# A ViT block on one NeuronCore: mask and row maximum in one VectorE instruction per head, in a reordered pipeline

## The chip, the cores and the metric

One NeuronCore of a Trainium2 chip runs the whole program; the other cores are idle. The metric is the device time of one execution in microseconds (us). Below, PE is TensorE, DVE is VectorE, ACT is ScalarE, POOL is GpSimd and SP is the engine that issues all DMAs. Each engine works through its own queue in order; semaphores tie the queues together.

## The reference: what is computed

Sixteen images of 256 by 256 pixels go through one block. The input is (16, 3, 256, 256) in fp32.

```python
gray  = einsum('bchw,c->bhw', x, (0.2989, 0.587, 0.114))
edges = conv 3x3 of gray with 2 Scharr filters, 'SAME'
h = abs(edges).sum(axis=1) / 2                       # (16, 256, 256)
xn = layernorm(h)                                    # no weights, eps 1e-5
Q = (xn @ W_dq @ W_uq) ; K = (xn @ W_dkv @ W_uk) ; V = (xn @ W_dkv @ W_uv)   # 16 heads of 16
scores = Q K^T / 4, causal, softmax over keys        # 256 x 256 per head
h = h + (softmax(scores) @ V) @ W_o
h = h + layernorm(h) @ sign(W_ffn).T
```

## The kernel before, in words

The unit of work is one image: 256 rows, as T = 2 tiles of 128 partitions. The 16 heads go in NG = 4 groups of G = 4. Queries and keys are cut into three bf16 parts each and stored so that six part products lie along the contraction (96 rows, KQ); three further rows (up to KM = 99) carry the row maximum, also in three parts, so that it is subtracted inside the product.

For each group the kernel does two things.

- **Query-major**, to find the maximum of each row: `hi_scores` (L836) gives queries 128 to 255 against all 256 keys, 4 heads, 1024 columns in two PSUM banks; `lo_scores` (L851) gives queries 0 to 127 against keys 0 to 127, 512 columns. A further product of a bf16 identity with a mask tile (`mask_qk`, L838 and L853) adds -3e38 above the diagonal. DVE then takes one `tensor_reduce` over 4 heads: `max_hi` (L668) and `max_lo` (L674). POOL cuts the maxima of 8 heads into parts (`cut_max`), PE transposes them (`turn_max`), ACT copies them and SP writes them into the operand (`load_max_rows`).
- **Key-major**, one image later: `key_scores_first` (L867, mask L869) and `key_scores_second` (L886), for keys 0 to 127 and 128 to 255. The second block has no mask product; DVE applies it with a minimum against a tile, in place in PSUM (`cap`, L679). ACT takes the exponential (`exp_first` L529, `exp_second` L534). `values` (L897, L900) multiplies with V, which carries a column of ones, so that the sum comes out too. ACT copies the result (L540), PE transposes it (`turn_output`, L926), DVE inverts the sums and multiplies (`normalize`, L686 and L689), PE transposes again (`turn_attn`), ACT copies (L545).

Around it stand, per image: gray (ACT L484, DVE L637 and L640), a store and a shifted reload through HBM, the filters (`filters`, L784), `both_edges` (ACT L490), the sum and statistics (DVE `sum_edges`, L646 to L654), the first normalization (POOL, L432 to L442), its transpose (`turn_x`), `compress` (L798), `expand_qk` (L807), `expand_v` (L817), the cut into parts (ACT L506 and L510, DVE L660, POOL `third_part` L462), a store and six reloads per half (`store_parts`, `load_operands`), and at the end `project` (L771), `add_y` (DVE L696 to L704), the second normalization (POOL, L447 to L457), `turn_y`, `feed_forward` (L771) and `add_z` (L709).

The order is written out by hand: a software pipeline over a step `i`, in which each engine works on several images at once. In step i, PE does scores of image i, key-major scores and values of i-1, the end of attention for i-2, projection for i-3, feed-forward for i-4, and the preparation of i+2 and i+3. Each step has four phases, one per head group.

## Time and profile before

| what | value |
|---|---|
| time, median of 3 runs | 512.27 us (504.1 to 512.48) |
| time of the profiled execution | 510.29 us |
| its span, first to last instruction | 508.4 us |
| mean granted TensorE clock | 0.946 of full speed |
| PE busy | 395.0 us (78%) |
| DVE busy | 289.1 us (57%) |
| ACT busy | 230.7 us (45%) |
| POOL busy | 163.7 us (32%) |
| DMA | 74.06 MB, mean 146 GB/s |

The profiled execution is 2.0 us under the median, and 1.9 us of it lie outside the span. Busy PE time is that of pipelined matmuls whose ends are modelled, so it overstates how full PE is.

### The profile page before, as it was taken

The numbers are of one execution on the slowest core, as the hardware profiler recorded it, in microseconds if no ns is written. First come the engines' busy times: TensorE is split into PE (matmuls) and PEld (weight loads), VectorE is DVE, ScalarE is ACT, GpSimd is POOL, SyncE is SP. The second block draws the span as 40 slices with busy tenths as digits, with TensorE's granted clock in tenths as the row PEclk, the third lists the DMA queues.
The fourth block names the chain that finished last, engine by engine and source line by source line (L and its number), as shares of the span: only waits on it lengthen the run. The fifth ranks groups of instructions, "written<-read, shape, count | busy, mean of one in ns | idle before, by whom it ended". The sixth has DMA issues, their size and how long they took to land.

```text
span 508.4 us, 10109 instructions
## 1 busy us (share of the span) xinstructions
PE 395.0 (78%) x3736; PEld 284.2 (56%) x3780; DVE 289.1 (57%) x508; ACT 230.7 (45%) x385; POOL 163.7 (32%) x363
## 2 busy tenths in 40 slices
PE   0047448586979898989898989898989899889863
PEld 0023335455656666666666666666666667666542
DVE  1422255574736667676666767676757576664321
ACT  2013123363635555555555555555555554446400
POOL 8220331413122424242424242424242422220111
PEclk9999569797979999999999999999999999999977
DMA  5954797675655666666767676737372425200000
GB/s 157 259 130 93 220 255 168 177 181 180 165 158 134 180 176 169 179 169 186 171 177 181 177 174 178 194 95 194 100 189 68 147 68 185 85 24 24 21 22 21
DMA packets 72186, 74.06 MB, mean 146 GB/s; under 512 B 6379, under 2 KB 65995, under 8 KB 72139
## 3 DMA queue, kind: packets, MB, share of 16 engines
q1 hardware_dynamic: 72138, 73.42, 53.6%
q8 instruction: 31, 0.51, 0.4%
q14 instruction: 17, 0.13, 0.1%
HBM read 51.97 MB, written 21.04 MB: 144 GB/s over the span
## 4 chain that ended last, share of the span: by engine, by line
PE 24%; POOL 23%; issue 22%; DVE 6%; ACT 1%; POOLq 0%
PE bank L771 9%; POOL parts L462 5%; POOL xn L442 4%; PE bank L764 3%; POOL yn L457 3%; PE bank L867 2%; POOL rstd L449 2%; DVE y L696 2%; PE bank L798 2%; PE bank L836 2%; POOL rstd L434 2%; DVE stats L700 1%; POOL max_rest L422 1%; POOL max_parts L427 1%; POOL max_parts L425 1%
## 5 line engine op out<-in xcount | busy, mean ns | idle before, releaser
L668 DVE TENSOR_REDUCE neg_max<-bank 128x4 f32<-128x1024 f32 x64 | 78.1, 1220 | 47.6 <-PE bank L838 46.6
L529 ACT ACTIVATE probs<-bank 128x1024 f32<-128x1024 f32 x64 | 65.6, 1025 | 63.3 <-PE bank L869 63.1
L462 POOL TENSOR_TENSOR parts<-rest,parts 128x1024 bf16<-128x1024 f32 x16 | 34.0, 2125 | 144.3 <-ACT parts L510 144.3
L784 PE MATMUL bank<-rows,band 102*32 102x256 f32 x512 | 34.3, 413 | 26.6 <-DMA rows<-gray_padded 25.7
L679 DVE TENSOR_TENSOR bank<-bank,cap_kq 128x512 f32<-128x512 f32 x64 | 44.4, 694 | 15.5 <-PE bank L886 15.5
L534 ACT ACTIVATE probs<-bank 128x512 f32<-128x512 f32 x64 | 38.2, 597 | 32.7 <-DVE bank L679 32.4
L836 PE MATMUL bank<-k_st,q_st 96*128 96x256 bf16 x256 | 48.6, 284 | 4.2 <-ACT edge L490 1.8
L867 PE MATMUL bank<-q_st,k_st 99*128 99x256 bf16 x256 | 47.5, 279 | 1.8 <-issue 0.2
L447 POOL TENSOR_SCALAR var<-mv 128x2 f32<-128x2 f32 x16 | 3.5, 219 | 133.3 <-DVE mv L704 133.3
L771 PE MATMUL bank<-w_sign,yn_t 128*128 128x256 f32 x128 | 35.1, 422 | 12.1 <-issue 9.9
L674 DVE TENSOR_REDUCE neg_max<-bank 128x4 f32<-128x512 f32 x64 | 43.6, 681 | 0.0
L764 PE MATMUL bank<-ident,xn 128*128 128x128 f32 x64 | 13.2, 341 | 37.5 <-POOL xn L442 37.5
L660 DVE TENSOR_TENSOR rest<-bank,parts 128x512 f32<-128x512 f32 x32 | 20.6, 686 | 35.8 <-ACT parts L506 35.8
L897 PE MATMUL bank<-probs,v_ring 128*32 128x256 f32 x512 | 40.6, 389 | 0.0
L540 ACT COPY o_un<-bank 128x256 f32<-128x256 f32 x64 | 23.6, 369 | 33.4 <-PE bank L900 33.4
L784 PEld LDWEIGHTS bank<-rows,band 102*32 102x32 f32 x512 | 16.3, 117 | 38.8 <-issue 30.5
L838 PE MATMUL bank<-mask_qk,ident_bf 128*128 128x256 bf16 x128 | 36.4, 285 | 0.0
L869 PE MATMUL bank<-mask_kq,ident_bf 128*128 128x256 bf16 x128 | 35.8, 280 | 0.0
L771 PEld LDWEIGHTS bank<-w_sign,yn_t 128*128 128x128 f32 x128 | 25.1, 207 | 18.2 <-issue 11.8
L771 PE MATMUL bank<-w_out,a_t 128*128 128x256 f32 x128 | 31.3, 387 | 1.4 <-ACT a_t L545 1.3
L867 PEld LDWEIGHTS bank<-q_st,k_st 99*128 99x128 bf16 x256 | 24.4, 100 | 13.0 <-issue 5.5
L490 ACT ACTIVATE edge<-bank 128x1024 f32<-128x1024 f32 x16 | 16.4, 1025 | 33.5 <-PE bank L784 33.5
(95 smaller groups left out, 768.8 us busy)
## 6 DMA issues: line engine op xcount, KB each, us to landing
x_sb<-in_x SPq DMA_DIRECT2D x16, 768.0 KB, 6.0
rows<-gray_padded SPq DMA_DIRECT2D x48, 256.0 KB
qk_parts<-parts SPq DMA_DIRECT2D x16, 768.0 KB, 4.1
q_st<-qk_parts SPq DMA_DIRECT2D x96, 128.0 KB, 3.9
k_st<-qk_parts SPq DMA_DIRECT2D x96, 128.0 KB, 3.6
gray_padded<-gray SPq DMA_DIRECT2D x16, 258.0 KB, 3.4
out_dram<-z SPq DMA_DIRECT2D x16, 256.0 KB, 2.5
rows<-gray_padded SPq DMA_DIRECT2D x32, 24.0 KB
```

What stands on the lines that cost most here:

```text
L462: pool.tensor_tensor(parts[:, n % 2, SLOTS_OF_PART[2], :, :], rest[:, :, :, :], parts[:, n % 2, SLOTS_OF_PART[1], :, :], ALU.subtract).the ...
L529: nc.scalar.activation(probs[:, g, :, 0:S], ps_k0, ACT.Exp, scale=SCALE).then_inc(exp0_done, 1)
L534: nc.scalar.activation(probs[:, g, :, S:S + P], ps_k1, ACT.Exp, scale=SCALE).then_inc(exp1_done, 1)
L668: nc.vector.tensor_reduce(neg_max[:, 1, heads], ps_hi, AX.X, ALU.max, negate=True).then_inc(max_hi_done, 1)
L674: nc.vector.tensor_reduce(neg_max[:, 0, heads], ps_lo, AX.X, ALU.max, negate=True).then_inc(max_lo_done, 1)
L679: nc.vector.tensor_tensor(ps_k1, ps_k1, cap_kq[:, :].unsqueeze(1).to_broadcast([P, G, P]), ALU.min).then_inc(capped, 1)
L771: last = nc.tensor.matmul(dst[:, t, :], src_t[:, c, t * P:(t + 1) * P], w[:, c, :], start=(c == 0), stop=(c == T - 1))
L784: last = nc.tensor.matmul(ps_edge[b * RB:(b + 1) * RB, t, f, :], band[0:KC, f, :], rows[0:KC, n % 2, t * (P // RB) + b, :], start=True, st ...
L836: nc.tensor.matmul(ps_hi[:, b * two + i, :], q[:, hh, P:S], k[:, hh, :], start=(i == 0), stop=False, skip_group_check=True)
L838: last = nc.tensor.matmul(ps_hi[:, b * two:(b + 1) * two, P:S], ident_bf[:, :], mask_qk[:, 0:two, :], start=False, stop=True, skip_group_c ...
L867: nc.tensor.matmul(ps_k0[:, i, :], k[:, hh, 0:P], q[:, hh, :], start=(i == b * two), stop=False, skip_group_check=True)
L897: nc.tensor.matmul(ps_o[i * VW:(i + 1) * VW, :], v_ring[:, n % V_RING, 0, g * G + i, :], probs[:, g, i, 0:S], start=True, stop=False, skip ...
```

## The change

Six things change together.

1. The mask products of the query-major scores go. Instead DVE runs one `tensor_tensor_reduce` per head: it adds a fp32 tile `mask_low` to the scores in place and gives the maximum of each row. That is 4 instructions in `max_hi` (256 columns each) and 4 in `max_lo` (128 each).
2. The mask of the second key block becomes a product on PE with `mask_kq` (512 columns) and `cap` goes.
3. After `values`, DVE transposes in blocks of 32 by 32 straight from PSUM (`turn_values`), inverts the sums, POOL multiplies (`normalize`), and DVE transposes back (`turn_attn`) into the operand of `project`. Heads are numbered by `head_of` so that this fits. PE's `turn_output` and `turn_attn` and ACT's five copies go.
4. The sum of the two edges moves from DVE to POOL. Both applications of the normalization (`xn`, `yn`) move from POOL to ACT. `both_edges` becomes two instructions, of half size.
5. PSUM: the small products now lie in banks 6 and 7 and no longer share banks with the scores, except for the filters, which still lie in the two banks of `ps_hi`.
6. The order of every queue changes and the tail is shorter: the attention of an image ends one step earlier, its projection too, and its feed-forward.

The new orders in step i (numbers in brackets are the image; a bar parts the phases):

- PE: key scores 0 [i-1], hi 0, lo 0 [i], values 3 [i-2], expand_v [i+1], turn_max 1 [i-1], turn_y [i-3] | key scores 1, hi 1, lo 1, values 0 [i-1], feed_forward [i-3], turn_x [i+2] | key scores 2, hi 2, lo 2, values 1 [i-1], project [i-2], turn_max 0 [i], compress [i+2] | key scores 3, hi 3, lo 3, values 2 [i-1], filters [i+3], expand_qk [i+2].
- DVE: rest_of_parts [i+1], max_hi 0, turn_values 3 and invert 1 [i-2], max_lo 0, measure_h [i+2] | max_hi 1, turn_values 0 [i-1], max_lo 1, turn_attn 1 [i-2] | rest_of_gray [i+4], add_z [i-3], max_hi 2, turn_values 1 and invert 0 [i-1], max_lo 2 | add_y [i-2], max_hi 3, turn_values 2 and turn_attn 0 [i-1], max_lo 3.
- ACT: exponentials 0 [i-1], second_part and copy_v [i+1], max rows 1 [i-1], copy_yt [i-3], normalize_x [i+2] | exponentials 1, first_gray [i+4], copy_xt [i+2] | exponentials 2, max rows 0 [i], copy_c [i+2] | exponentials 3, both_edges [i+3], normalize_y [i-2], first_part [i+2].
- POOL: cut_max 1 [i-1], sum_edges and scale_x [i+2], normalize 1 [i-2], third_part [i+1], cut_max 0 [i], normalize 0 [i-1], scale_y [i-2].
- SP: load_rows [i+3], max rows 1 [i-1], store_parts and load_operands 0 [i+1], store_z [i-3], max rows 0 [i], store_gray [i+4], load_x [i+6], load_operands 1 [i+1]. The weights are loaded behind the first rows, no longer ahead of the first gray image.

In the diff the common indent is cut, and lines left out are marked.

```diff
--- before.py
+++ after.py
...
-FIRST = -6
-LAST = IMAGES + 4
+FIRST = -4
...
+def head_of(g, i):
+    return (g // 2) * HALF + g % 2 + 2 * i
...
+    def sum_edges(n):
+        pool.wait_ge(abs_done, T * (n + 1))
+        need(pool, y_done, upto(n - H_RING))
+        need(pool, xn_done, T * upto(n - H_RING))
+        pool.tensor_tensor(h_ring[:, n % H_RING, :, :], edge[:, :, 0, :], edge[:, :, 1, :],
+                           ALU.add).then_inc(h_done, 1)
...
+    def scale_x(n):
...
+        pool.tensor_scalar(less[:, :], mv[:, :, 0], -1.0, None, ALU.mult).then_inc(less_done, 1)
...
+        pool.wait_ge(less_done, n + 1)
+        pool.tensor_tensor(shift[:, :], less[:, :], rstd[:, :], ALU.mult).then_inc(shift_done, 1)
...
+    def normalize(n, c):
+        k = T * n + c + 1
+        pool.wait_ge(recip_done, k)
+        need(pool, at_done, k - T)
+        pool.tensor_tensor(attn[:, c, :, :, :].rearrange("p q x d -> p x q d"), u[:, c, :, :, 0:DK],
+                           recip[:, c, :, :].unsqueeze(3).to_broadcast([P, 2, NQ, DK]),
+                           ALU.mult).then_inc(attn_done, 1)
...
     def both_edges(n):
-        act.wait_ge(filters_done, T * (n + 1))
         need(act, h_done, n)
-        nc.scalar.activation(edge[:, :, :, :], ps_edge, ACT.Abs).then_inc(abs_done, 1)
+        for t in range(T):
+            act.wait_ge(filters_done, T * n + t + 1)
+            nc.scalar.activation(edge[:, t, :, :], ps_edge[:, t, :, :], ACT.Abs).then_inc(abs_done, 1)
+    def normalize_x(n):
+        act.wait_ge(shift_done, n + 1)
+        need(act, xt_done, n)
+        for t in range(T):
+            nc.scalar.activation(xn[:, t, :], h_ring[:, n % H_RING, t, :], ACT.Identity,
+                                 bias=shift[:, t:t + 1], scale=rstd[:, t:t + 1]).then_inc(xn_done, 1)
...
     def exp_second(n, g):
         at = NG * n + g
-        act.wait_ge(capped, at + 1)
+        act.wait_ge(k1_done, at + 1)
...
-    def copy_o(n, g):
-        act.wait_ge(o_done, NG * n + g + 1)
-        if g == 0:
-            need(act, ot_done, T * (n - 1))
-        nc.scalar.copy(o_un[:, n % 2, g, :], ps_o).then_inc(o_copied, 1)
-    def copy_at(n):
-        act.wait_ge(at_done, n + 1)
-        need(act, proj_done, n)
-        nc.scalar.copy(a_t[:, :, :], ps_at).then_inc(at_copied, 1)
...
     def max_hi(n, g):
-        heads = slice(g * G, (g + 1) * G)
         if g % 2 == 0:
             need(dve, cut[1], 2 * n - 1 + g // 2)
         dve.wait_ge(hi_done, NG * n + g + 1)
-        nc.vector.tensor_reduce(neg_max[:, 1, heads], ps_hi, AX.X, ALU.max,
-                                negate=True).then_inc(max_hi_done, 1)
+        for i in range(G):
+            last = nc.vector.tensor_tensor_reduce(ps_hi[:, i, :], ps_hi[:, i, :], mask_low[:, :], 1.0, MASK,
+                                                  ALU.add, ALU.max,
+                                                  top[:, 1, g // 2, i, g % 2].unsqueeze(1))
+        last.then_inc(max_hi_done, 1)
     def max_lo(n, g):
-        heads = slice(g * G, (g + 1) * G)
         dve.wait_ge(lo_done, NG * n + g + 1)
-        nc.vector.tensor_reduce(neg_max[:, 0, heads], ps_lo, AX.X, ALU.max,
-                                negate=True).then_inc(max_lo_done, 1)
-    def cap(n, g):
-        dve.wait_ge(k1_done, NG * n + g + 1)
-        nc.vector.tensor_tensor(ps_k1, ps_k1, cap_kq[:, :].unsqueeze(1).to_broadcast([P, G, P]),
-                                ALU.min).then_inc(capped, 1)
-    def normalize(n, t):
-        k = T * n + t + 1
-        o = ps_ot.rearrange("p (h d) -> p h d", d=VW)
-        dve.wait_ge(ot_done, k)
-        nc.vector.reciprocal(recip[:, t, :], o[:, :, DK]).then_inc(recip_done, 1)
-        dve.wait_ge(recip_done, k)
-        need(dve, at_done, n)
-        nc.vector.tensor_tensor(attn[:, t, :].rearrange("p (h d) -> p h d", d=DK), o[:, :, 0:DK],
-                                recip[:, t, :].unsqueeze(2).to_broadcast([P, H, DK]),
-                                ALU.mult).then_inc(attn_done, 1)
+        for i in range(G):
+            last = nc.vector.tensor_tensor_reduce(ps_lo[:, i, :], ps_lo[:, i, :], mask_low[:, P:S], 1.0, MASK,
+                                                  ALU.add, ALU.max,
+                                                  top[:, 0, g // 2, i, g % 2].unsqueeze(1))
+        last.then_inc(max_lo_done, 1)
+    def turn_values(n, g):
+        c, x = g // 2, g % 2
+        dve.wait_ge(o_done, NG * n + g + 1)
+        need(dve, attn_done, T * (n - 1) + c + 1)
+        nc.vector.transpose(u[:, c, x, :, :].rearrange("p q d -> p (q d)"), ps_o).then_inc(o_turned, 1)
+    def invert(n, c):
+        dve.wait_ge(o_turned, NG * n + 2 * c + 2)
+        nc.vector.reciprocal(recip[:, c, :, :], u[:, c, :, :, DK]).then_inc(recip_done, 1)
+    def turn_attn(n, c):
+        dve.wait_ge(attn_done, T * n + c + 1)
+        need(dve, proj_done, n - 1)
+        nc.vector.transpose(a_t[:, n % 2, c, :],
+                            attn[:, c, :, :, :].rearrange("p q x d -> p (q x d)")).then_inc(at_done, 1)
...
-        need(pe, y_done, upto(n - 6))
-        need(pe, z_done, upto(n - 7))
...
     def turn_x(n):
         pe.wait_ge(xn_done, T * (n + 1))
-        need(pe, attn_done, T * upto(n - 5))
-        need(pe, v_copied, n)
+        need(pe, o_turned, NG * upto(n - 4) + (1 if live(n - 3) else 0))
+        need(pe, rest_done, 2 * n)
         turn(ps_xt, xn, xt_done)
...
     def expand_qk(n):
         pe.wait_ge(c_copied, n + 1)
-        need(pe, exp0_done, NG * upto(n - 4) + (3 if live(n - 3) else 0))
-        need(pe, rest_done, 2 * n)
+        need(pe, o_turned, NG * upto(n - 4) + (3 if live(n - 3) else 0))
+        need(pe, v_copied, upto(n - 1))
+        need(pe, y_done, upto(n - 4))
...
     def expand_v(n):
         pe.wait_ge(c_copied, n + 1)
-        need(pe, attn_done, T * upto(n - 5) + (1 if live(n - 4) else 0))
...
         need(pe, max_hi_done, NG * n + g)
         if g == 0:
-            need(pe, abs_done, upto(n + 2))
-        if g == 1:
-            need(pe, z_done, upto(n - 4))
-        if g == 2:
-            need(pe, y_done, upto(n - 3))
-        for b in range(2):
-            for i in range(two):
-                hh = g * G + b * two + i
-                nc.tensor.matmul(ps_hi[:, b * two + i, :], q[:, hh, P:S], k[:, hh, :],
-                                 start=(i == 0), stop=False, skip_group_check=True)
-            last = nc.tensor.matmul(ps_hi[:, b * two:(b + 1) * two, P:S], ident_bf[:, :],
-                                    mask_qk[:, 0:two, :], start=False, stop=True,
-                                    skip_group_check=True)
+            need(pe, abs_done, T * upto(n + 2))
+        for i in range(G):
+            hh = head_of(g, i)
+            last = nc.tensor.matmul(ps_hi[:, i, :], q[:, hh, P:S], k[:, hh, :], start=True, stop=True)
         last.then_inc(hi_done, 1)
     def lo_scores(n, g):
         q = q_st[0:KQ, n % 2, :, :]
         k = k_st[0:KQ, n % 2, :, :]
         need(pe, max_lo_done, NG * n + g)
-        if g == 1:
-            need(pe, at_copied, upto(n - 3))
         for i in range(G):
-            hh = g * G + i
-            nc.tensor.matmul(ps_lo[:, i, :], q[:, hh, 0:P], k[:, hh, 0:P],
-                             start=(i == 0), stop=False, skip_group_check=True)
-        nc.tensor.matmul(ps_lo[:, :, :], ident_bf[:, :], mask_qk[:, :, :], start=False, stop=True,
-                         skip_group_check=True).then_inc(lo_done, 1)
+            hh = head_of(g, i)
+            last = nc.tensor.matmul(ps_lo[:, i, :], q[:, hh, 0:P], k[:, hh, 0:P], start=True, stop=True)
+        last.then_inc(lo_done, 1)
...
-        if g == 0:
-            need(pe, yt_copied, upto(n - 3))
         if g == 1:
             need(pe, mt_copied, 2 * (n + 1))
         if g == 3:
             need(pe, mt_copied, 2 * (n + 1) + (1 if live(n + 1) else 0))
         for i in range(G):
-            hh = g * G + i
-            last = nc.tensor.matmul(ps_k1[:, i, :], k[:, hh, P:S], q[:, hh, P:S],
-                                    start=True, stop=True)
-        last.then_inc(k1_done, 1)
+            hh = head_of(g, i)
+            nc.tensor.matmul(ps_k1[:, i, :], k[:, hh, P:S], q[:, hh, P:S],
+                             start=(i == 0), stop=False, skip_group_check=True)
+        nc.tensor.matmul(ps_k1[:, :, :], ident_bf[:, :], mask_kq[:, :, :], start=False, stop=True,
+                         skip_group_check=True).then_inc(k1_done, 1)
...
             pe.wait_ge(v_copied, n + 1)
         pe.wait_ge(exp1_done, at + 1)
-        need(pe, o_copied, at)
+        need(pe, o_turned, at)
+        if g == 0:
+            need(pe, yt_copied, upto(n - 2))
+        if g == 1:
+            need(pe, xt_copied, upto(n + 3))
+        if g == 2:
+            need(pe, c_copied, upto(n + 3))
+        if g == 3:
+            need(pe, rest_done, 2 * upto(n + 3))
         for i in range(G):
...
-    def turn_output(n, t):
-        if t == 0:
-            pe.wait_ge(o_copied, NG * (n + 1))
-            need(pe, c_copied, upto(n + 4))
...
-                                       o_un[:, n % 2, g, t * P:(t + 1) * P], ident[:, :])
-        last.then_inc(ot_done, 1)
-    def turn_attn(n):
-        pe.wait_ge(attn_done, T * (n + 1))
-        need(pe, max_lo_done, NG * upto(n + 2) + (1 if live(n + 3) else 0))
-        turn(ps_at, attn, at_done)
     def project(n):
-        pe.wait_ge(at_copied, n + 1)
-        need(pe, max_hi_done, NG * upto(n + 2) + (2 if live(n + 3) else 0))
+        pe.wait_ge(at_done, T * (n + 1))
         need(pe, z_done, upto(n - 1))
-        need(pe, abs_done, upto(n + 5))
-        product(ps_y, a_t, w_out, proj_done)
+        need(pe, v_copied, upto(n + 3))
+        product(ps_y, a_t[:, n % 2, :, :], w_out, proj_done)
...
     def turn_y(n):
         pe.wait_ge(yn_done, T * (n + 1))
-        need(pe, exp1_done, NG * upto(n + 2))
+        need(pe, o_turned, NG * upto(n + 1))
         turn(ps_yt, yn, yt_done)
```

## Rows read from the trace of the kernel before

**Rows 1.** Chain that ended last, in time order: start us, us, what; two steps.

```profile
243.37 2.12 POOL parts L462
...
253.90 1.80 PE bank L771 x8
...
269.17 2.12 POOL parts L462
```

**Rows 2.** Windows: us, busy (x instructions) of PE, PEld, DVE, ACT, POOL; clock, DMA, GB/s.

```profile
0.00:67.60 67.60, 23.82 (x150) 13.66 (x151) 19.65 (x39) 14.20 (x21) 23.46 (x41) 0.92 0.67 175
...
202.80:301.60 98.80, 87.66 (x902) 63.98 (x912) 68.51 (x122) 55.19 (x93) 37.76 (x84) 1.00 0.68 180
...
457.00:508.40 51.40, 36.47 (x270) 25.24 (x268) 16.19 (x36) 14.68 (x25) 8.20 (x22) 0.87 0.06 22
```

**Rows 3.** Groups by line, DVE: count, busy us, mean ns, idle before.

```profile
L668 DVE TENSOR_REDUCE neg_max<-bank 128x4 f32<-128x1024 f32 x64 | 78.1, 1220 | 47.6 <-PE bank L838 46.6
...
L679 DVE TENSOR_TENSOR bank<-bank,cap_kq 128x512 f32<-128x512 f32 x64 | 44.4, 694 | 15.5 <-PE bank L886 15.5
L674 DVE TENSOR_REDUCE neg_max<-bank 128x4 f32<-128x512 f32 x64 | 43.6, 681 | 0.0
...
L689 DVE TENSOR_TENSOR attn<-bank,recip 128x256 f32<-128x256 f32 x32 | 13.6, 424 | 1.2
...
L646 DVE TENSOR_TENSOR h_ring<-edge 128x512 f32<-128x512 f32 x16 | 11.1, 692 | 35.5 <-ACT edge L490 35.5
```

**Rows 4.** Timeline, DVE: start us, us, instructions, idle before. Pairs without a wait between.

```profile
256.44 0.75 DVE L700 BATCH_NORM_STATS2 stats<-y 128x6 f32<-128x256 f32 x2
257.12 0.30 DVE L704 BATCH_NORM_AGGREGATE mv<-stats 128x2 f32<-128x6 f32 x2
```

**Rows 5.** Groups by line: the small DVE operations that pair up in rows 4.

```profile
L700 DVE BATCH_NORM_STATS2 stats<-y 128x6 f32<-128x256 f32 x32 | 12.0, 418 | 0.5
...
L704 DVE BATCH_NORM_AGGREGATE mv<-stats 128x2 f32<-128x6 f32 x32 | 4.8, 173 | 0.0
```

**Rows 6.** Timeline, PE only, 258.33 to 267.03: start us, us, instructions.

```profile
258.33 0.60 PE L926 MATMUL bank<-ident,o_un 128*128 128x128 f32 x4
258.76 0.39 PE L886 MATMUL bank<-q_st,k_st 99*128 99x128 bf16 x4
...
259.87 1.13 PE L807 MATMUL bank<-c_t,w_qk 64*128 64x256 f32 x8
...
261.82 0.28 PE L838 MATMUL bank<-mask_qk,ident_bf 128*128 128x256 bf16 x1
261.93 0.27 PE L836 MATMUL bank<-k_st,q_st 96*128 96x256 bf16 x1
...
264.85 1.93 PE L784 MATMUL bank<-rows,band 102*32 102x256 f32 x32
266.60 0.62 PE L897 MATMUL bank<-probs,v_ring 128*32 128x256 f32 x8
```

**Rows 7.** Groups by line, ACT and POOL.

```profile
L529 ACT ACTIVATE probs<-bank 128x1024 f32<-128x1024 f32 x64 | 65.6, 1025 | 63.3 <-PE bank L869 63.1
...
L534 ACT ACTIVATE probs<-bank 128x512 f32<-128x512 f32 x64 | 38.2, 597 | 32.7 <-DVE bank L679 32.4
...
L540 ACT COPY o_un<-bank 128x256 f32<-128x256 f32 x64 | 23.6, 369 | 33.4 <-PE bank L900 33.4
...
L434 POOL TENSOR_TENSOR rstd<-var,power 128x2 f32<-128x2 f32 x16 | 12.7, 793 | 1.3
```

**Rows 8.** Timeline, PE, from the end of the last key scores on.

```profile
473.84 0.63 PE L764 MATMUL bank<-ident,yn 128*128 128x128 f32 x4
...
481.57 0.40 PE L900 MATMUL bank<-probs,v_ring 128*32 128x128 f32 x8
...
492.75 1.99 PE L771 MATMUL bank<-w_out,a_t 128*128 128x256 f32 x8 [0.68 <-ACT a_t L545]
...
501.22 3.78 PE L771 MATMUL bank<-w_sign,yn_t 128*128 128x256 f32 x8 [0.68 <-ACT yn_t L550]
```

481 lines of the change are left out of this document (239 added, 242 removed).

## The prediction

> **What bounds the kernel now.** I read the page's busy shares first. PE is busy 78% of the span, DVE 57%, ACT 45%, POOL 32%. Over four steps in the middle PE is busy 87.7 of 98.8 us, DVE 68.5, ACT 55.2, POOL 37.8, at the full clock of 2.4 GHz [rows 2]. So PE is nearly full, and DVE is at 69%.
>
> Then the chain of waits. It repeats: the same piece of POOL (`third_part`) stands at 243.37 and at 269.17 [rows 1], so a step takes **25.8 us** in the middle of the run. The chain runs through POOL, PE and DVE. PE's busy share times the step is 0.887 x 25.8 = 22.9 us; about 3 us per step PE waits. The first maximum is at 67.6 us, the last at about 457, and from there 51.4 us remain, in which DMA and DVE are nearly idle [rows 2]. The change touches the step, which counts 15.75 times (63 group intervals of a quarter step), and the tail.
>
> **Step by step, per image (one step), in the middle.**
>
> *PE.* A mask product of 256 columns costs one issue interval: L838 starts at 261.82, the next product at 261.93, 0.11 us [rows 6]. Eight go: -0.88. The 512-column mask of the low scores goes and one of the same size comes in the second key block: 0. `turn_output` issues for 258.76 - 258.33 = 0.43 us, twice, and `turn_attn` is as many transposes again, once: -1.29. Together -2.2, so PE needs 22.9 - 2.2 = **20.7 us**. PE stops being the bound if anything else needs more.
>
> *DVE, what goes.* `max_hi` 78.1, `max_lo` 43.6, `cap` 44.4, the multiplication of `normalize` 13.6 and the edge sum 11.1 [rows 3] are 190.8 us, 11.9 per image. DVE is busy 289.1 in all; 98.3 are left, 6.1 per image. Groups that overlap at their ends are counted once in the total and twice in the groups, so this is a little low; I take 6.5.
>
> *DVE, what comes.* Six transposes of 128 by 256. No row shows a transpose; the nearest is an operation over 256 fp32 columns, 0.418 us alone and 0.33 us as the second of a pair (0.75 - 0.42) [rows 4, 5]. 6 x 0.42 = 2.5. The inversion stays.
>
> Then 32 fused instructions. The rate is 1.05 ns per column in the rows: the 1024-column maximum takes 1220 ns and the 512-column one 681, so 512 columns cost 539 ns [rows 3]; `cap`, which has two inputs and writes PSUM in place as the new instruction does, takes 694 for 512 [rows 3]. So 16 x (0.267 + 0.133) = 6.4 us of columns, and a **fixed cost f** 32 times. f is the whole question. DVE's sum is D = 6.5 + 2.5 + 6.4 + 32 f = 15.4 + 32 f.
>
> Bounds of f. Below: the pair in rows 4 starts its second instruction 0.33 us after the first, for 0.267 of columns, so f = 0.065, if bringing out the maximum costs nothing. Above: the instruction's whole duration counts, 0.418 - 0.267 = 0.151, and the result comes out in a further small operation at the full price of the smallest DVE row, 0.173 [rows 5]: f = 0.324. The value: instructions without a wait between them do overlap in this trace, so 0.065, plus a further small one at pair price, 0.30 - 0.17 = 0.13 [rows 4, 5]. **f = 0.2**, D = 21.8 us.
>
> The Trainium skill, "VectorE: DVE Perf Modes", section "Two Vector instructions with no wait between them", says that an operation that also writes out its accumulator is two instructions. Nothing of it shows in this trace, in which no operation has such an output. The same page, section "The DRAIN you can't avoid", says that the next operation does not start until the pipe is empty, and leaves out those that nothing holds back. Held, the 32 pairs would make the sum that of f = 0.324; a held pair in rows 4 would take 0.84 us, and it takes 0.75, so the trace shows the exception there.
>
> *Two gaps on DVE that the new order leaves.* PE starts `filters` [i+3] only when max_hi 3 has read the banks; then `expand_qk`; then ACT's `first_part`, queued behind the edges and `normalize_y`; then DVE's `rest_of_parts`, the first thing of its next step. From the end of max_hi 3: filters issue 1.75 at most (266.60 - 264.85), here 1.6, expand_qk 1.13 [rows 6]; ACT by then has one half of the edges behind it, then two copies of 0.369 for `normalize_y` and the first half of 0.597 [rows 7]: about 4.0 us. DVE has work for two transposes and max_lo 3: 0.84 + 0.53 + 4 f. Gap 1 = 2.6 - 4 f = 1.8 us.
>
> The second: `measure_h` on DVE, then POOL `scale_x` (the power 0.793 and three small ones, 1.75), ACT `normalize_x` 2 x 0.37, exponentials 1.025 + 0.597, gray 0.6 [rows 7], and only then `rest_of_gray`: 4.8 us. DVE in between: max_hi 1, max_lo 1 and two transposes, 2.4 + 8 f. Gap 2 = 2.4 - 8 f = 0.8 us. Queued behind ACT's wait for `scale_x` are the exponentials of group 1, and behind them PE's key scores 2; the same sum shows that they come before DVE wants hi 2.
>
> So the step is D + gaps = 20.4 + 20 f = **24.4 us** against 25.8. Over 15.75 steps: -22 us.
>
> *ACT and POOL.* ACT loses five copies per image (4 x 0.369 and one of the 0.597 kind [rows 7]) and gains four of 0.37 and one more fixed part; it stays near 14.9 of 24.4. POOL loses four multiplications over 256 columns and gains the edge sum and two multiplications of that kind. Both have more than 9 us to spare and cost nothing but the chain above. If D fell under PE's 20.7, PE would be the bound, not they.
>
> *SP.* Same transfers, same bytes. `load_rows` goes first in the step and max rows ahead of the gray store; both wait for less than before. 0.
>
> *Tail.* Before, values 3 of the last image waited behind turn_y, feed-forward and projection of older images, which began at 473.84; its second half starts at 481.57 and its first 0.4 earlier [rows 8]. In the new order it comes first: -7.3. From its end (481.97) to the last `project` (492.75) were 10.8 us with copies, eight PE transposes and another feed-forward; now five short operations of under 0.6 each on DVE and POOL run beside one feed-forward, about 4 us: -6.8. From project to feed-forward 8.5 us [rows 8], now some 0.6 less. Together **-15**.
>
> *Ramp.* Weights behind the first rows bring them sooner; `filters` of image 1 now goes before `expand_qk` of image 0 on PE, and at the low clock. Between -6 and +5; I take 0.
>
> **Sum.** 510.3 - 22 - 15 = **473 us**, on the scale of the profiled execution, which is 0.4% under the median of the runs shown; I say 474.
>
> **Rivals.**
>
> - *A. The fused instruction is dear: nothing overlaps.* f = 0.324, D = 25.8, gap 1 = 1.3, gap 2 = 0: step 27.1, +20.5, with the tail 516 us. For it: every instruction has an output of its own to bring out, and many small pieces pay the fixed part each. The Trainium skill, "VectorE: DVE Perf Modes", section "The TRN2 errata", says the same in general: "a single large tile pays it once; many small tiles pay it per-tile". Against it: rows 4. It lies within 2% of 512 for f between 0.29 and 0.34. Chance 0.15.
> - *B. Slower: the fused instruction runs at half rate*, since it reads PSUM and SBUF, writes PSUM and keeps a running maximum. Columns then cost 12.8 instead of 6.4, D = 28.2 at f = 0.2, gap 1 = 1.3: step 29.5, +58, 553 us. It is slower than 522 from about 1.5 times the price of a column on. Against it: `cap` ran in place at full rate [rows 3]. Chance of this side 0.17, of it 0.05 for f above 0.34 and 0.04 for a clock that falls to 1.2 GHz in gap 1, where it costs 3 us a step.
> - *C. The gain of the step does not come*, because another loop closes at 25.8 us (POOL's chain takes on the edge sum and the multiplications): 510.3 - 15 = 495. Against it: the chain of rows 1 is cut by moving `third_part` and the normalizations. Chance 0.13.
> - *D. f near its lower bound*: 0.065 gives a step of 21.7 and 431 us; at f = 0.117 it is 445. Chance of under 455: 0.15.
>
> **Numbers.** About 2% can be told from no change here: 502 and 522.5. My forecast, 455 to 485, has 0.40; D 0.15; C and what lies up to 502, 0.13; together faster 0.68. A gives 0.15 within 2%, B and what goes with it 0.17 slower. The range is 445 to 520: it takes in C and A, leaves about 0.08 below and 0.12 above (with the ramp's -6 to +5 inside it).
>
> **What would show it.** DVE becomes the busiest engine after PE, over 80% in the middle, with two groups of 256 instructions at 0.4 to 0.5 us and 0.25 to 0.4; a further row for bringing out the maximum, if there is one. The start of one max_hi of group 3 to the next gives the step. `rest_of_parts` waits for ACT about 1.8 us and `rest_of_gray` about 0.8. PE waits before `filters` for max_hi 3. L838, L926 and the transposes of `turn_attn` are gone. The tail from the last max_hi to the end is about 36 us. I am wrong if a column costs more than 1.05 ns, if f is outside 0.12 to 0.29, or if POOL's rows end DVE's waits.

## The result, and the profile after

The changed kernel takes **462.38 us** (median; 455.24 to 468.7) against 510.48 for the kernel before on the same chip: a ratio of 0.9045, 95% interval 0.8749 to 0.9342. Two of the four runs of each kernel were more than 1.5% above its fastest, and all ratios leave such slow runs out, while the medians are over all runs. In a later job it was 463.47, ratio 0.9127 (0.9035 to 0.922). I had said 474 us.

The page of after: span, busy shares, clock and DMA in 40 slices.

```profile
span 462.1 us, 10365 instructions
PE 364.4 (79%) x3428; PEld 255.8 (55%) x3460; DVE 302.1 (65%) x1387; ACT 228.9 (50%) x385; POOL 164.6 (36%) x345
PEclk9976655969999999999999899999999999959996
DMA  4976495965494959496949693867465525430000
PE 40%; DMA 21%; SPq 13%; issue 8%; DVE 8%; POOL 5%; ACT 4%; POOLq 0%; ACTq 0%; DVEq 0%
DMA q_st<-top_rows 9%; SPq L310 9%; DMA qk_parts<-parts 8%; PE bank L813 7%; PE bank L824 5%; PE bank L930 5%; PE bank L893 4%; PE bank L872 4%; POOL parts L444 3%; DVE rest L690 3%; PE bank L839 3%; PE bank L858 2%; PE bank L806 2%; PE bank L910 2%; PE bank L933 2%
```

Windows of after (us, busy time and instructions of PE, PEld, DVE, ACT, POOL, then clock, DMA share, GB/s), cut as in [rows 2] at the first and the last `max_hi`.

```profile
0.00:59.40 59.40, 21.91 (x139) 11.38 (x140) 16.02 (x31) 16.09 (x26) 22.54 (x37) 0.81 0.66 170
202.80:301.60 98.80, 87.57 (x880) 63.52 (x887) 75.89 (x360) 57.64 (x100) 38.73 (x81) 0.98 0.74 193
426.20:462.10 35.90, 22.47 (x176) 15.71 (x178) 11.56 (x38) 11.31 (x18) 5.75 (x17) 0.87 0.07 23
```

The ledger of the spans: ahead of the first maximum 59.4 us against 67.6, -8.2; the 15.75 steps 366.8 against 389.4, -22.6; the tail 35.9 against 51.4, -15.5. Together -46.3, which is 508.4 - 462.1.

The groups of after that answer to [rows 3, 5, 7], by line, with count, busy us, mean ns and idle time before.

```profile
L698 DVE CUSTOM_DVE_ANT_0 bank<-bank,mask_low 128x256 f32<-128x256 f32 x256 | 100.9, 457 | 43.4 <-PE bank L872 43.4
L706 DVE CUSTOM_DVE_ANT_0 bank<-bank,mask_low 128x128 f32<-128x128 f32 x256 | 65.1, 318 | 0.0
L690 DVE TENSOR_TENSOR rest<-bank,parts 128x512 f32<-128x512 f32 x32 | 20.6, 686 | 51.9 <-ACT parts L547 51.9
L698 DVE DVE_READ_ACCUMULATOR2_ANT top<- 128x1 f32 x256 | 36.6, 143 | 0.0
L706 DVE DVE_READ_ACCUMULATOR2_ANT top<- 128x1 f32 x256 | 36.4, 142 | 0.0
L530 ACT ACTIVATE xn<-h_ring,shift,rstd 128x256 f32<-128x256 f32 x32 | 17.5, 592 | 34.9 <-POOL shift L429 34.9
```

The maximum does come out in a second instruction (`DVE_READ_ACCUMULATOR2_ANT`), 143 ns, one per head. How the two fit together, and the wait that the new order leaves (`rest_of_parts`, L690), the timeline of DVE shows:

```profile
268.37 0.47 DVE L698 CUSTOM_DVE_ANT_0 bank<-bank,mask_low 128x256 f32<-128x256 f32 x1
268.75 0.14 DVE L698 DVE_READ_ACCUMULATOR2_ANT top<- 128x1 f32 x1
268.75 0.47 DVE L698 CUSTOM_DVE_ANT_0 bank<-bank,mask_low 128x256 f32<-128x256 f32 x1
269.13 0.14 DVE L698 DVE_READ_ACCUMULATOR2_ANT top<- 128x1 f32 x1
...
270.25 0.33 DVE L706 CUSTOM_DVE_ANT_0 bank<-bank,mask_low 128x128 f32<-128x128 f32 x1
270.50 0.14 DVE L706 DVE_READ_ACCUMULATOR2_ANT top<- 128x1 f32 x1
270.50 0.33 DVE L706 CUSTOM_DVE_ANT_0 bank<-bank,mask_low 128x128 f32<-128x128 f32 x1
270.75 0.14 DVE L706 DVE_READ_ACCUMULATOR2_ANT top<- 128x1 f32 x1
273.51 1.29 DVE L690 TENSOR_TENSOR rest<-bank,parts 128x512 f32<-128x512 f32 x2 [2.62 <-ACT parts L547]
```

The read starts at the same moment as the next head, so the price is in the spacing and not in the rows' lengths: 0.38 us from one 256-column head to the next, 0.247 for 128 columns.

Now the steps. The start of `rest_of_parts` marks them. Two in a row, with the same columns as the windows above:

```profile
224.18:246.88 22.70, 20.83 (x215) 15.14 (x217) 18.28 (x87) 13.99 (x25) 9.67 (x20) 1.00 0.68 179
246.88:273.51 26.63, 22.28 (x215) 16.04 (x217) 18.38 (x86) 14.08 (x25) 9.67 (x20) 0.94 0.82 216
```

**There are two kinds of step.** An undisturbed one takes 22.70 us, to 0.01 us, again and again. In between stand longer ones of 23 to 26.6 us, with a DMA share of 0.73 to 0.82. What is late in the longest of them PE shows (start, us, instruction, idle before), with SP's issues ahead of it:

```profile
258.55 0.61 PE L893 MATMUL bank<-q_st,k_st 99*128 99x256 bf16 x2 [2.61 <-DMA q_st<-top_rows]
```

```profile
244.08 0.46 SPq L269 DMA_DIRECT2D x_sb<-in_x  x1
244.64 2.85 SPq L310 DMA_DIRECT2D q_st<-qk_parts  x3
247.53 1.86 SPq L310 DMA_DIRECT2D k_st<-qk_parts  x3
249.49 1.51 SPq L287 DMA_DIRECT2D rows<-gray_padded  x3
251.05 0.68 SPq L291 DMA_DIRECT2D rows<-gray_padded  x2
251.78 0.81 SPq L317 DMA_DIRECT2D q_st<-top_rows  x1
```

The 12 KB of maximum rows are issued at 251.78 behind 2.3 MB of other transfers (768 KB pixels, six operand loads of 128 KB, three row loads of 256 KB), and key scores 2 gets them 6.8 us later. After that wait the product takes 0.61 us instead of 0.38: PE stood still for 2.6 us, and the granted clock of that step is 0.94.

### The profile page after: what moved, and what is told of

Read it like the earlier page. It is cut to its first block, busy times and chain, and to the rows that moved or that the text cites. A ratio compares the mean times of both kernels' runs of the same rounds, so it can differ in the third digit from the quotient of the medians.

```text
span 462.1 us, 10365 instructions
## 1 busy us (share of the span) xinstructions
PE 364.4 (79%) x3428; PEld 255.8 (55%) x3460; DVE 302.1 (65%) x1387; ACT 228.9 (50%) x385; POOL 164.6 (36%) x345
## 4 chain that ended last, share of the span: by engine, by line
PE 40%; DMA 21%; SPq 13%; issue 8%; DVE 8%; POOL 5%; ACT 4%; POOLq 0%; ACTq 0%; DVEq 0%
DMA q_st<-top_rows 9%; SPq L310 9%; DMA qk_parts<-parts 8%; PE bank L813 7%; PE bank L824 5%; PE bank L930 5%; PE bank L893 4%; PE bank L872 4%; POOL parts L444 3%; DVE rest L690 3%; PE bank L839 3%; PE bank L858 2%; PE bank L806 2%; PE bank L910 2%; PE bank L933 2%
## 5 line engine op out<-in xcount | busy, mean ns | idle before, releaser
L698 DVE CUSTOM_DVE_ANT_0 bank<-bank,mask_low 128x256 f32<-128x256 f32 x256 | 100.9, 457 | 43.4 <-PE bank L872 43.4
L706 DVE CUSTOM_DVE_ANT_0 bank<-bank,mask_low 128x128 f32<-128x128 f32 x256 | 65.1, 318 | 0.0
L824 PE MATMUL bank<-rows,band 102*32 102x256 f32 x512 | 37.5, 442 | 33.3 <-DMA rows<-gray_padded 22.6
L893 PE MATMUL bank<-q_st,k_st 99*128 99x256 bf16 x256 | 48.8, 285 | 16.2 <-DMA q_st<-top_rows 15.8
L690 DVE TENSOR_TENSOR rest<-bank,parts 128x512 f32<-128x512 f32 x32 | 20.6, 686 | 51.9 <-ACT parts L547 51.9
L872 PE MATMUL bank<-k_st,q_st 96*128 96x256 bf16 x256 | 41.9, 289 | 7.2 <-DMA k_st<-qk_parts 5.0
L524 ACT ACTIVATE edge<-bank 128x512 f32<-128x512 f32 x32 | 19.1, 597 | 51.5 <-PE bank L824 51.5
L468 POOL TENSOR_TENSOR attn<-u,recip 128x256 f32<-128x256 f32 x32 | 19.8, 620 | 68.4 <-DVE recip L719 68.4
L893 PEld LDWEIGHTS bank<-q_st,k_st 99*128 99x128 bf16 x256 | 23.3, 101 | 29.8 <-DMA q_st<-top_rows 19.7
L698 DVE DVE_READ_ACCUMULATOR2_ANT top<- 128x1 f32 x256 | 36.6, 143 | 0.0
L706 DVE DVE_READ_ACCUMULATOR2_ANT top<- 128x1 f32 x256 | 36.4, 142 | 0.0
L872 PEld LDWEIGHTS bank<-k_st,q_st 96*128 96x128 bf16 x256 | 26.2, 103 | 17.2 <-DMA k_st<-qk_parts 5.8
L530 ACT ACTIVATE xn<-h_ring,shift,rstd 128x256 f32<-128x256 f32 x32 | 17.5, 592 | 34.9 <-POOL shift L429 34.9
L564 ACT COPY top_rows<-bank 24x256 bf16<-24x256 bf16 x32 | 11.5, 359 | 43.8 <-PE bank L947 43.8
```

Source lines behind the costliest of these rows:

```text
L698: last = nc.vector.tensor_tensor_reduce(ps_hi[:, i, :], ps_hi[:, i, :], mask_low[:, :], 1.0, MASK, ALU.add, ALU.max, top[:, 1, g // 2, i, ...
L706: last = nc.vector.tensor_tensor_reduce(ps_lo[:, i, :], ps_lo[:, i, :], mask_low[:, P:S], 1.0, MASK, ALU.add, ALU.max, top[:, 0, g // 2, i ...
L824: last = nc.tensor.matmul(ps_edge[b * RB:(b + 1) * RB, t, f, :], band[0:KC, f, :], rows[0:KC, n % 2, t * (P // RB) + b, :], start=True, st ...
L872: last = nc.tensor.matmul(ps_hi[:, i, :], q[:, hh, P:S], k[:, hh, :], start=True, stop=True)
L893: nc.tensor.matmul(ps_k0[:, i, :], k[:, hh, 0:P], q[:, hh, :], start=(i == b * two), stop=False, skip_group_check=True)
```

## The experiments

The theory after the first look, **L**: a chain through DVE, ACT and PE makes the step of 22.7 us, in which the two gaps stand, and late maximum rows add about 1 us on average. Its first rival, **D**: DVE's own time is the bound. A further one, **P**: PE's is. Later **T**: the rows are late by their place in SP's queue; and **T2**: they are late by the bytes in flight ahead of them. Times are medians; the ratio is to the kernel before in the same job. To compare steps I give the undisturbed step, and the mean over nine steps from about 130 us to about 345 us.

**The changed kernel once more**, as the base of all the others.

> The changed kernel once more, beside the three below on the same chip. Theory and rival alike: 455 to 469 us, as in its runs so far. It is the reference for the others.

463.47 us, span 461.2. The nine steps from 128.93 to 341.98 have a mean of 23.67 us, the short ones are 22.70. It is as expected.

**The old order with the new masks.**

```diff
-                nc.vector.tensor_reduce(neg_max[:, 1, heads], ps_hi, AX.X, ALU.max,
-                                        negate=True).then_inc(max_hi_done, 1)
+                for i in range(G):
+                    last = nc.vector.tensor_tensor_reduce(ps_hi[:, i, :], ps_hi[:, i, :], mask_low[:, :], 1.0, MASK,
+                                                          ALU.add, ALU.max,
+                                                          neg_max[:, 1, g * G + i].unsqueeze(1))
...
-            def cap(n, g):
...
-            pool.memset(k_st[KQ:KM, :, :, :], 1.0).then_inc(ones_set, 1)
+            pool.memset(k_st[KQ:KM, :, :, :], -1.0).then_inc(ones_set, 1)
```

> The kernel before, in its old order, with only the masks changed: one fused VectorE instruction per head for mask and maximum, no mask products in the query-major scores, the mask of the second key block as a product on TensorE, no minimum on VectorE. Theory (the new order and the moved work bring the gain, the fused instruction alone brings little): VectorE takes 10.0 us per image for the maxima instead of 7.0 and loses 2.8 of the minimum, TensorE loses 0.9, and the old loop through GpSimd stays closed: 490 to 510 us. Rival (the masks bring the gain): under 475 us.

500.88 us, ratio 0.9908 (0.9856 to 0.9959), as the theory had it. So the fused masks and the second block's mask on PE, in the old order, are worth 1% together.

**The new order with the old masks**: two mask products on PE again and one `tensor_reduce` per group; the second key block keeps its mask on PE.

```diff
-                for i in range(G):
-                    last = nc.vector.tensor_tensor_reduce(ps_hi[:, i, :], ps_hi[:, i, :], mask_low[:, :], 1.0, MASK,
-                                                          ALU.add, ALU.max,
-                                                          top[:, 1, g // 2, i, g % 2].unsqueeze(1))
-                last.then_inc(max_hi_done, 1)
+                nc.vector.tensor_reduce(top[:, 1, g // 2, :, g % 2], ps_hi, AX.X, ALU.max).then_inc(max_hi_done, 1)
...
+                    last = nc.tensor.matmul(ps_hi[:, b * two:(b + 1) * two, P:S], ident_bf[:, :],
+                                            mask_qk[:, 0:two, :], start=False, stop=True,
+                                            skip_group_check=True)
```

> The changed kernel with the query-major masks back as products on TensorE and one reduction over four heads on VectorE, all else as changed. Theory (VectorE and its two gaps set the step of 22.7 us): VectorE loses 3.0 us a step and the gaps grow by 1.1, so it would allow 20.8, but TensorE goes to about 22.4 issue-bound: the step stays within 1 us of 22.7, 450 to 472 us. Rival (TensorE already sets the step): +1.7 us a step, about 490 us.

**454.96 us**, ratio 0.8992 (0.892 to 0.9065), inside the theory's range and far from the rival's 490: not slower than the fused form, by the medians 8 us faster. (The two intervals just overlap; in the job that timed both, its four runs end at 457.13 and those of the changed kernel begin at 459.4.) The windows of a step:

```profile
221.52:244.50 22.98, 22.59 (x230) 16.18 (x229) 15.73 (x30) 14.21 (x25) 9.70 (x20) 1.00 0.67 171
```

PE 22.6 of 22.98 us, DVE 2.55 us less. Its undisturbed step is 0.28 us longer, and yet the mean of nine steps is 23.46, shorter than 23.67. Waits for the maximum rows are 2.7 us from 150 to 350 us, against 10.3. So the fused instruction does not carry the gain; the rest of the change does, that is the order, the DVE transposes, the moved work and the banks together. Of these only the second block's mask is tried alone below; the others were not split. What is lost in the short step is paid back in the long ones, which neither D nor P explains. Only 1.9 of the 8.8 us between the two spans lie in the nine steps; where most of the rest lies is said behind the run with the rows from ACT.

**The second key block's mask back on DVE** (`cap`, a minimum in place after each key scores), in the new order.

```diff
...
+            def cap(n, g):
+                dve.wait_ge(k1_done, NG * n + g + 1)
+                nc.vector.tensor_tensor(ps_k1, ps_k1, cap_kq[:, :].unsqueeze(1).to_broadcast([P, G, P]),
+                                        ALU.min).then_inc(capped, 1)
...
```

> The changed kernel with the mask of the second key block back as a minimum on VectorE (ahead of the maximum of its group), without its product on TensorE. Theory (VectorE sets the step): +2.5 us of VectorE a step, in none of the two gaps: +35 to +45 us, about 500. Rival (TensorE sets it): -0.85 a step, about 450.

467.38 us, ratio 0.9222 (0.9136 to 0.9308): both theories missed. The windows:

```profile
229.84:253.98 24.14, 20.15 (x213) 14.51 (x212) 20.45 (x90) 14.30 (x25) 9.68 (x20) 1.00 0.72 182
253.98:278.12 24.14, 20.37 (x216) 14.82 (x214) 20.45 (x91) 14.40 (x25) 9.67 (x20) 1.00 0.72 187
```

DVE has 2.17 us more to do, and the short step is 1.44 longer; DVE's waits for `hi_scores` are gone (0.3 us from 150 to 350, against 14.6). But most steps are now short ones. A longer step gives the traffic more time; the rows are less late (6.7 us of waits, against 10.3), and the mean is 24.36, only 0.7 over 23.67.

**PE made dearer, DVE left alone**: products with a tile of zeros where the masks had been.

```diff
+                    last = nc.tensor.matmul(ps_hi[:, b * two:(b + 1) * two, P:S], ident_bf[:, :],
+                                            blank[:, 0:two, :], start=False, stop=True,
+                                            skip_group_check=True)
...
+                nc.tensor.matmul(ps_lo[:, :, :], ident_bf[:, :], blank[:, :, :], start=False, stop=True,
+                                 skip_group_check=True).then_inc(lo_done, 1)
```

> The kernel after, with 1,024 more columns of mask products per group added to the query-major scores on PE with a tile of zeros (two products of 256 columns in hi_scores, one of 512 in lo_scores), exactly those that the kernel before had there; DVE keeps its fused instructions. So PE has about 1.7 us more per image (4 x 1,024 columns at about 0.42 ns), DVE nothing more. Theory L (the step is a chain that passes through DVE, PE and ACT in turn, in which PE stands only with hi_scores ahead of max_hi and DVE waits for PE some times in a step): the products delay hi_done and lo_done by 0.2 us each time, 8 times in a step, of which half falls on the chain, so +0.8 us in each of 15.75 steps: 475 us (469 to 483). Rival D (DVE alone sets the step): no change, 461 to 466 us. Rival P (PE alone sets the step): +1.7 us x 15.75 = +27 us: 486 to 494 us.

464.21 us, ratio 0.919 (0.9107 to 0.9272), no change against the base, and P is out. By the windows the case is the same as with `cap`:

```profile
272.88:296.27 23.39, 22.59 (x230) 16.18 (x229) 18.28 (x86) 14.00 (x25) 9.68 (x20) 1.00 0.69 176
296.27:321.28 25.01, 22.76 (x230) 16.12 (x229) 18.37 (x86) 14.10 (x25) 9.68 (x20) 1.00 0.76 200
```

1.7 us more PE work, 0.69 us more in the short step (L had said 0.8), and waits for the rows of 2.7 us instead of 10.3. The mean of nine steps grew by 0.19 only, and another 4 us were given back in the last steps, as shown below. D's number was met, but not D's reason: the short step did grow.

**The gaps made smaller**: two swaps in ACT's queue.

```diff
+                if live(i + 4):
+                    first_gray(i + 4)
                 if live(i + 2):
                     normalize_x(i + 2)
...
+                if live(i + 2):
+                    first_part(i + 2)
                 if live(i - 2):
                     normalize_y(i - 2)
```

> The kernel after, with two swaps in the queue of ACT: first_part ahead of normalize_y in phase 4, and first_gray ahead of normalize_x in phase 2. Nothing is added. Theory L (the two gaps, DVE's wait of 2.6 us for rest_of_parts behind normalize_y, and of 0.9 us for rest_of_gray behind normalize_x, lie on the chain of each step): the first gap shrinks by the 1.1 us of the two normalize_y instructions, the second by 0.9, so -2.0 us in each of 15.75 steps at most, and -1 where another wait comes up behind: 432 to 449 us, I take 441. Rival P (PE, or the late maximum rows, sets the step by itself; the gaps are only where DVE waits for it): 457 to 466 us, no change.

467.59 us, ratio 0.9114 (0.898 to 0.9248): L missed, no change. Yet the short step did shrink:

```profile
229.61:251.63 22.02, 20.83 (x217) 15.01 (x215) 18.66 (x86) 14.03 (x25) 9.69 (x21) 1.00 0.60 155
251.63:279.67 28.04, 23.94 (x222) 16.74 (x220) 19.05 (x87) 14.03 (x25) 9.71 (x21) 0.88 0.80 206
```

22.02 instead of 22.70. The second gap is gone; the first fell only from 2.6 to 2.3, because `first_part` now waits 0.5 us for `expand_qk` on PE. But the long steps grew to 28.0 us at a granted clock of 0.88. A shorter step meets the same traffic earlier. (The profile is of the execution of 471.99 us, of runs between 458.44 and 471.99, so the short step is what I use.)

**The maximum rows from another queue.**

```diff
-                if live(i - 1):
-                    load_max_rows(i - 1, 1)
...
-                if live(i):
-                    load_max_rows(i, 0)
...
+                act.wait_ge(mt_copied, 2 * n + hf + 1)
+                act.dma_start(q_st[KQ:KM, n % 2, hf * HALF:(hf + 1) * HALF, :],
+                              top_rows[:, :]).then_inc(row_in[hf], 16)
```

> The kernel after, with the transfer of the maximum rows issued from ACT's queue right behind ACT's own copy, no longer from SP's queue, where it stands behind row loads and operand loads. Theory T (key scores 2 waits 1.4 to 2.9 us in every second step for this transfer, and 1.0 us of the mean step of 23.6 us is this wait): the steps lose what lies above 22.7 us, 15.75 x 0.9 = 14 us less: 445 to 454 us. Rival (the transfer itself is slow, by the load of the DMA queues, and not its place in SP's order; or what is taken away comes up as another wait, as with the extra DVE time of the run with cap): 459 to 467 us, with the waits for the rows still in the trace or other ones in their place.

456.2 us, ratio 0.8942 (0.8821 to 0.9064), between the two forecasts. PE still waits 7.8 us for the rows from 150 to 350 us (10.3 in the base), and the mean of nine steps is 23.39. One case, the issue on ACT's queue and the wait of PE:

```profile
224.48 0.73 ACTq L562 DMA_DIRECT2D q_st<-top_rows  x1
```

```profile
231.83 0.39 PE L892 MATMUL bank<-q_st,k_st 99*128 99x256 bf16 x2 [2.54 <-DMA q_st<-top_rows]
```

7.35 us from issue to use, although nothing stood ahead of it in the queue that issued it. SP had issued 3.6 MB in the 12 us before, and those bytes are left as the likely cause; here SP's order was not. That is the ground for T2.

At the end of the run it was. From the start of the last `rest_of_parts` to the last `max_hi` the base and this kernel compare so:

```profile
385.33:425.40 40.07, 35.03 (x334) 25.18 (x335) 29.05 (x147) 17.56 (x27) 9.66 (x26) 0.91 0.32 97
```

```profile
379.65:412.60 32.95, 31.35 (x327) 22.72 (x325) 28.75 (x145) 17.29 (x27) 9.63 (x26) 1.00 0.38 115
```

In the base, SP has six operand loads and a store ahead of the rows; ACT has copied them by 402.24, SP issues them at 404.21, and PE stands still:

```profile
404.21 0.81 SPq L317 DMA_DIRECT2D q_st<-top_rows  x1
```

```profile
407.51 0.46 PE L893 MATMUL bank<-q_st,k_st 99*128 99x256 bf16 x2 [3.01 <-DMA q_st<-top_rows]
```

From ACT's queue the same transfer is issued 0.04 us after the copy, and used 2.67 us later after a wait of 0.44. This stretch alone gives 7.1 of the 12.3 us between the two spans. It splits all kernels in two: where its granted clock is 1.00 it takes 33.0 to 35.9 us (rows from ACT, alone, with the swaps and with all; unfused masks; more PE work; pixels later with the swaps), and where it is 0.83 to 0.91 it takes 37.8 to 40.1 us (the changed kernel twice, `cap`, the swaps, pixels later, no pixels). For the unfused masks it is 34.37, 5.7 us of their 8.8.

**The gaps and the queue together** (both edits).

> The kernel after, with both edits together: first_part ahead of normalize_y, first_gray ahead of normalize_x, and the maximum rows sent from ACT's queue. If the gaps and the late rows are separate losses on one chain, the gains add: 20.8 to 21.7 us a step, 425 to 437 us. If the rows' wait only takes up slack that the gaps leave, the result is that of the better one of the two alone. If PE's own 20.7 us a step with its clock below full is the floor, 440 to 450 us.

458.4 us, ratio 0.9073 (0.8993 to 0.9153). Short steps of 22.03 to 22.12 and long ones of 25.6 to 26.1 take turns, with a mean of 23.73. The gains do not add: this is the better one of the two alone, not their sum.

**The pixels loaded later**, out of the heap ahead of the maximum rows.

```diff
                 if live(i - 1):
                     load_max_rows(i - 1, 1)
+                if live(i + 5) and i + 5 >= 2:
+                    load_x(i + 5)
...
-                if live(i + 6):
-                    load_x(i + 6)
```

> The kernel after, with the load of an image's 768 KB of pixels moved in SP's queue: not ahead of the second half of the operand loads and of the row loads, with which it makes 2.3 MB in one go just ahead of the maximum rows, but behind the maximum rows, ahead of store_parts of the next step, where SP now waits for POOL and the trace shows 0 to 60 GB/s for 2 us. Theory T2 (the late maximum rows are late by the bytes that are queued ahead of them on all DMA engines, not by SP's order): 768 KB less ahead at 250 to 300 GB/s is 2.6 to 3 us less, so key scores 2 waits no more, and all steps go to 22.7 us: 446 to 455 us, I take 450. Rival (the pixels now delay store_parts and the reload of the operands by the same 3 us, and hi_scores of the next image waits for them): 460 to 475 us, with waits of PE for k_st or q_st from qk_parts in every step.

457.83 us, ratio 0.9016 (0.8953 to 0.9079). Waits for the rows fall from 10.3 to 4.8 us and the mean step from 23.67 to 23.10; so T2 missed its range of 446 to 455 us, though it had the direction right. PE's waits for the operands did not come.

**No pixels at all** after the first two images: 11 MB of 74 less.

```diff
-                if live(i + 6):
-                    load_x(i + 6)
...
-                act.wait_ge(x_in[n % 2], 16 * (n // 2 + 1))
+                act.wait_ge(x_in[n % 2], 16)
```

> The kernel after without the loads of the pixels of images 2 to 15 (the gray images are computed from whatever lies in the two buffers): 11 MB of 74 MB less to move, everything else as it was. Theory T2: the steps of 23.5 to 26.6 us vanish, 22.7 us each, and the ramp may gain 0 to 4 us: 443 to 453 us. Rival (what makes a step longer than 22.7 us is not the DMA load): 459 to 467 us. With e8_x_later it tells how much of the traffic's cost the move alone takes away.

**449.44 us**, ratio 0.8871 (0.8801 to 0.894). T2 is met. (The images 2 to 15 are computed from stale pixels, so this is no version to use.) Its windows:

```profile
215.14:237.83 22.69, 20.93 (x218) 15.13 (x217) 18.29 (x86) 13.98 (x25) 9.66 (x20) 1.00 0.60 166
237.83:260.71 22.88, 20.99 (x218) 15.12 (x217) 18.28 (x86) 14.09 (x25) 9.68 (x20) 1.00 0.62 174
```

The same instructions on PE, DVE and ACT, only bytes are gone, and seven of the nine steps are 22.69 or 22.70 us, the mean 22.78. So the pixels' traffic costs 0.9 us a step in the middle. The span is 14.4 us shorter, and 13.2 of them lie between the first and the last `max_hi`.

**The pixels later and the two swaps.**

> The kernel after with the pixels loaded later, as in e8_x_later, and the two swaps in ACT's queue of e4_act_order. In e4_act_order every second step was 22.02 us against 22.70, and the others grew to 24 to 28 us with the late rows and a lower clock. Theory (the gaps do set the short step; the gain was given back because a faster step meets the same traffic): with the traffic out of the way all steps are 22.0 us, 0.7 us x 15.75 = 11 us under e8_x_later: 434 to 445 us. Rival (each step cannot go under about 23.5 us on average by the DMA's own throughput): the same as e8_x_later or slower, 450 to 462 us.

**453.75 us**, ratio 0.8941 (0.888 to 0.9001), as the rival, a floor set by the traffic, had it. Two of the nine steps are 22.02, one is 25.90 at a clock of 0.93, and the mean is 23.14, as without the swaps (23.10). What it gains on the pixels alone lies at the end: its last stretch takes 35.26 us, against 38.79.

**All three edits.**

> The kernel after with all three edits that need no change of the arithmetic: the two swaps in ACT's queue, the maximum rows sent from ACT's queue, and the pixels loaded behind the maximum rows. Alone or in pairs they gave 467.6 (swaps), 456.2 (rows from ACT), 457.8 (pixels later), 458.4 (swaps and rows) and 453.8 us (swaps and pixels). If the edits to the traffic add up (each took 6 to 9 us), the remaining waits for the rows shrink below 0.3 us a step and the steps come near 22.1 us: 440 to 449 us, I take 446, the fastest of all. If the traffic's average is a floor of about 23 us a step whatever the order, 451 to 457 us.

455.97 us, ratio 0.8983 (0.8904 to 0.9061), mean step 23.56: in the range of the floor, and not the sum of the gains. The rows' own queue adds nothing to the kernel with pixels later and swaps, whose last stretch was already at the full clock. The same without the swaps was not run.

Of versions that do the full work, 453.75 to 456.2 us is the best group (pixels later with the swaps; the unfused masks; the rows from ACT; all three). It beats the kernel before by 10 to 11%. Within the group, and for most of it against the changed kernel too, the intervals overlap.

## Why the prediction was right, and where it was wrong

**The step before.** I took 25.8 us from one distance in the chain [rows 1]. The mean of the run is 389.4 / 15.75 = 24.7, and the window of [rows 2] says the same: 98.8 us for four steps. The profile had it; I read one disturbed step as the rule. PE's need, 22.9, was worked out with it and should have been 21.9.

**PE after: 20.7 us.** Measured 20.8 to 21.0 in an undisturbed step. From the right base the same -2.2 would have given 19.7, so PE lost only about 1.1 us, and two errors cancel. Mask products put back cost 1.65 us in the run with more PE work, close to what my price gives for their 4,096 columns (1.8); so the shortfall is not there. That leaves the transposes, which no run tries alone.

**The fixed cost f, 0.2 us.** Measured from the spacings of heads: with 0.267 and 0.133 us for the columns as I had them, 0.38 - 0.267 = 0.113 and 0.247 - 0.133 = 0.114. That is just outside the 0.12 to 0.29 of my own sign of being wrong. The columns' rate was right (1.04 ns), the accumulator's read was there (143 ns, predicted 130 as a further small instruction), but I charged it in full; it overlaps the next head. The Trainium skill, "VectorE: DVE Perf Modes", section "Two Vector instructions with no wait between them", calls such an operation two instructions, and the trace agrees: 512 further rows. What it costs, 0.05 us over my lower bound, only the spacing shows. DVE comes to 77% of the middle window (75.9 of 98.8), not to over 80%.

**The step: 20.4 + 20 f.** With f = 0.114 it gives 22.7, and the undisturbed step is 22.70. The agreement is partly luck, for its terms are off both ways. Gap 1 was 2.62, not 1.8 (2.1 by my formula at the measured f): `normalize_y` is an activation with a scale and a shift, 0.59 us where I took 0.37 from a copy [rows 7], so its pair takes 1.08, and `filters` issues for 1.86 us, not 1.6. Gap 2 was 0.92, which looks like my 0.8, but at the measured f my formula gives 1.5. Besides, DVE waits for `hi_scores`, which I had at nothing: 0.49 and 0.24 us in the undisturbed step from 273.51 on, and 14.6 us in 200 with the long steps. Against it stands DVE's own time, 18.3 busy where the formula has 19.05. The experiments show the same: 2.17 us more on DVE cost 1.44, 1.7 us more on PE cost 0.69, smaller gaps gave 0.68. The step is a chain that changes engines, not one engine's sum.

**SP and DMA: 0. Here the mechanism was wrong.** "Same transfers, same bytes" is true, but in a shorter step the same bytes come closer together: 193 GB/s in the middle against 180 in [rows 2], and a 12 KB transfer that PE needs at once stands behind 2.3 MB. It costs 0.9 us a step in the middle, by the run without pixels, and "both wait for less than before" was wrong too: no wait of PE for the maximum rows shows in the kernel before, 15.8 us of them in the one after, and in the last steps SP issues the rows 2 us late. Over all 15.75 steps the mean is 23.3 (366.8 / 15.75), in which the shorter steps near the end count as well: -22.6 us. I had -22: from a base 1.1 too high to a step 1.1 too high. That the term of the steps fits is luck.

**Tail, -15**: -15.5. Right, and by its parts, last `max_hi` to end, 35.9 us (I had said about 36).

**Ramp, 0**: -8.2, outside my -6 to +5. PE's timeline splits it. `filters` of image 0 starts at 22.57 us instead of 25.73 (-3.2); SP now issues the weights behind the first rows. `turn_x` of image 0 starts at 32.05 instead of 36.57 (-1.4 more), that of image 1 at 46.92 instead of 56.12 (-4.7 more); 1.0 is lost again up to the first maximum. Ahead of the `turn_x` of image 1, PE waited for POOL before and waits for ACT after:

```profile
56.12 1.11 PE L764 MATMUL bank<-ident,xn 128*128 128x128 f32 x4 [7.94 <-POOL xn L442]
```

```profile
46.92 1.11 PE L806 MATMUL bank<-ident,xn 128*128 128x128 f32 x4 [2.36 <-ACT xn L530]
```

I had priced the move of the normalization only in the steady step. The ramp is most of the 11 us that I was off. Its parts are read from the timelines; no run tries them alone.

**The rivals.** A and B fell with f = 0.114 and a column at 1.04 ns. C, that another loop closes at 25.8, did not come in that form, but the traffic, which I had not named, took some 13 us. D was right on the instruction. Its number at f = 0.117 was given as 445 us; by its own sum it is 447. Nothing that does the full work reaches it: the wrong base and the traffic stand between.

**Open.** Which transfer of the heap is last to give way to the 12 KB was not separated, nor whether the shorter step or the new order brought the rows' waits. What tips the last stretch to the lower clock was followed in the base only. Nor was the ramp of the variants, which differs by up to 10 us from one to the other. That the traffic is a floor under the average is argued, not shown: no run takes the pixels away and makes the swaps too. The granted clock has a part in it, since the long steps of the swapped kernels at 0.93 have 22.6 us of PE busy time where their short ones have 20.9.

## What to carry to other kernels

Take the step time as a mean over the whole loop, never from one distance in the chain: the disturbed steps are in it too. And compare the end of the loop as well as its middle: here it held 3.5 to 7 us of the differences between variants. When compute per step shrinks, ask which small, urgent transfer stands behind large ones that could wait, and try that by taking bytes away: when each change to an engine moves the short step but not the total, something else sets the average. A change of order that carries along a new instruction must be split: here the masks alone gave 1% in the old order, all the rest of the change 8 to 10%, and the fused instruction in the new order nothing, or a small loss.
